# Biases of the first layer's MLP moved into the setup, and the input added by the third norm

## The chip, the cores and the metric

The kernel runs on one core of one Trainium2 chip. Time is device microseconds of one execution of the whole program; three runs of the kernel before lie between 2295.13 and 2299.04 us, the median is 2298.62. The core's engines are PE (TensorE), DVE (VectorE), ACT (ScalarE), POOL (GpSimd) and SP (SyncE, which only issues transfers). Each engine takes its instructions in order and waits on semaphores for the others.

## The reference, cut to what matters

Four layers of different kinds run one after the other over 8192 rows of 256 values (128 graphs of 64 nodes). The change is in the first:

```python
x1 = relu(_layernorm((L_norm @ x) @ Wc + bc, g1, be1)) + x
o  = attention(x1 @ Wq, x1 @ Wk, x1 @ Wv, adjacency)
x2 = _layernorm(x1 + o @ Wo + bo, g2, be2)
m  = gelu(x2 @ W1 + b1) @ W2 + b2
h  = _layernorm(x2 + m, g3, be3)
x  = _layernorm(x + h)              # of the stack, without weights
```

L_norm comes from a 64x64 matrix whose largest eigenvalue is found by 24 squarings.

## The kernel before

**Setup (lines 448 to 641).** SP loads weights and vectors. PE and DVE pass a 64x64 matrix back and forth: PE squares it (L624), DVE copies it back (L585), and after every fourth squaring, a run, PE sums a trace with a 64x128 by 64x1 product (L627) and DVE scales by its reciprocal (L581, L587). There are six runs. What DVE computes from the result (lnormT, ahatT and two rows of biases, L601 to L609) ends the setup, and a barrier of all engines follows.

**First layer (lines 644 to 947).** The rows are cut into 32 groups of 256, two 128-row tiles each. Four streams, 0 to 3, take 8 groups each, one per turn. The work on a group is a list of numbered slots:

- slot 0 and 1: product with lnormT, product with Wc (L864), add bc (L812) and statistics of the first norm (L344 bn_stats, L348 bn_aggr, two of each); POOL makes rstd (L356 and L358)
- slot 2: affine of the first norm on DVE, two L386 `(y - mean) * g` and two L391 `y * rstd + be`, one per tile, then relu and residual (L819)
- slot 3: PE transposes (L887), ACT copies the result as a rounded high part (L758), DVE makes the rest (the split, L802); POOL adds bo to x1 in a 128x512 add (L738)
- slots 4 to 10: query, key and value products in three passes (L323), scores, softmax (L823, L827 to L831 on DVE), product with the values
- slots 11 and 12: product with Wo, sum with L738's result (L836), statistics, rstd on POOL, affine of the second norm (L386 and L391 again)
- slot 13: PE transposes the second norm's result (L887), split as before; POOL adds b2 to it (L742, 128x512)
- slots 14 and 15: product with W1, gelu with b1_col as bias on ACT, product with W2, sum with L742's result (L845), statistics of the third norm
- slot 16: affine of the third norm on DVE; then POOL adds the layer's input, which SP loads again in slot 4 (L706), in a 128x512 add (L746)
- slot 17: statistics of the stack's norm on DVE, rstd and shift on POOL (L365 to L370); slot 18: ACT applies them (L376), SP stores (L709)

What runs on an engine when is set by plan0, a table that gives each slot of each engine a tick. The period is 88 ticks, the streams are shifted by lead = (0, 13, 19, 31), and weave writes the instructions of all streams out in the order of (tick - lead) modulo 88; the ticks set the order alone, not a time. PE, DVE, ACT, POOL and SP each follow their own list and meet by semaphores.

Of the kernel before, what the change touches and what calls it, by code (L numbers as in the profile page):

```python
# [122 lines left out]
def build_program(nc, ctx, t, out_rows):  # L123
# [258 lines left out]
    def ln_affine(dve, c, y, s, g, be, ready, rstd, count, ready_count=None):  # L382

        dve.wait_ge(ready, count if ready_count is None else ready_count)
        for n in range(TILES):
            c.step(dve.scalar_tensor_tensor(out=y[:, n, :], in0=y[:, n, :], scalar=ln_mv[:, s, n, 0:1], in1=g,  # L386
                                            op0=ALU.subtract, op1=ALU.mult))
        c.settle()
        dve.wait_ge(rstd, count)
        for n in range(TILES):  # L390
            ins = dve.scalar_tensor_tensor(out=y[:, n, :], in0=y[:, n, :], scalar=ln_rstd[:, s, n:n + 1], in1=be,  # L391
                                           op0=ALU.mult, op1=ALU.add)
            if n < TILES - 1:
                c.step(ins)
        return ins
# [47 lines left out]
    w0_hi = psem("w0_hi")  # L443
    pool_steps, sums_asked, spread_asked = psem("pool_steps"), psem("sums_asked"), psem("spread_asked")
# [3 lines left out]
    with nc.Block() as block:  # L448

        @block.sync  # L450
        def _(sp):
# [87 lines left out]
        def _(dve):  # L539
# [66 lines left out]
            dve.wait_ge(spread_done, 1)  # L606
            link(dve.tensor_tensor(ahatT[:], abdT, ps0(0)[:, 0:P], ALU.mult))
# [5 lines left out]
        def _(pe):  # L613
# [6 lines left out]
            with pe.Fori(0, SQUARINGS // RUN) as i:  # L620
                for r in range(RUN):
                    pe.wait_ge(p_ready, RUN * i + r + 1)
                    alone(pe, waits_passed)
                    pe.matmul(ps0(3)[0:NODES, 0:NODES], P64[0:NODES], P64[0:NODES], start=True, stop=True)\  # L624
                      .then_inc(squared, 1)
                pe.wait_ge(q_ready, i + 1)
                pe.matmul(ps0(4)[:, 0:1], ones[0:NODES, :], col[0:NODES, 12:13],  # L627
                          start=True, stop=True).then_inc(tr_ready, 1)
# [43 lines left out]
    def up_ps(s):  # L672
# [6 lines left out]
     atT_ready, up_done, gelu_ready, var2_ready, rstd2_ready, y_made, yx_ready, y_ready, y_stored) = (sems(n) for n in  # L679
# [3 lines left out]
                   "up_done", "gelu_ready", "var2_ready", "rstd2_ready", "y_made", "yx_ready", "y_ready",  # L683
# [6 lines left out]
        dve={1: 26, 2: 31, 3: 35, 6: 51, 8: 60, 11: 77, 12: 80, 13: 85, 15: 100, 16: 104, 17: 111},  # L690
        pool={1: 29, 3: 45, 11: 78, 13: 80, 15: 104, 16: 108, 17: 119},
        sp={2: 56, 4: 68, 18: 122})

    with nc.Block() as block:

        @block.sync
        def _(sp):
            ahead(sp, y_stored, by=16)

            def stage(s, slot, turn):  # L700
# [3 lines left out]
                if slot == 4:  # L704
                    sp.wait_ge(yx_ready[s], turn + 1)
# [87 lines left out]
        def _(dve):  # L793
            steps = Steps(dve, "l0_dve", {1: 1 + LN_STATS, 2: LN_AFFINE, 8: 2, 11: 1 + LN_STATS,
                                          12: LN_AFFINE - 1})
            tail = Steps(dve, "l0_dve_tail", {15: 1 + LN_STATS, 16: LN_AFFINE - 1, 17: LN_STATS})
            ahead(dve, var2_ready, by=2)

# [6 lines left out]
            def stage(s, slot, turn):  # L805
# [9 lines left out]
                if slot == 2:  # L815
                    c.step(ln_affine(dve, c, hb_t[s], s, g1, be1, var_ready[s], rstd_ready[s], 2 * turn + 1))
# [22 lines left out]
                if slot == 12:  # L839
                    ln_affine(dve, c, hb_t[s], s, g2, be2, var_ready[s], rstd_ready[s], 2 * turn + 2)\  # L840
# [1002 lines left out]
```

## Time and profile before

| what | value |
|---|---|
| median of three runs | 2298.62 us |
| span of the profiled execution, which is all of its time that the record gives | 2298.5 us |
| setup, to the first product of the layer | 0 to 43.0 us |
| first layer, to its last apply on ACT | 43.0 to 684.0 us |
| PE busy over the span | 2138.9 us (93%) |
| DVE busy | 1384.4 us (60%) |
| POOL busy | 440.6 us (19%) |

Busy is the share of the span in which an engine works on an instruction. A wait is the idle time just before an instruction, with the instruction of the other engine that released it. In the timeline "x2" stands for two instructions that follow one another, and the time is that of both. A pass is one of the matmul instructions into which PE takes a product.

### The profile page before, as it was taken

To read this page: it belongs to the slowest core of one execution; us is meant where nothing else is said; L and a number is where in the kernel's file an instruction comes from. 1 tells how busy PE (TensorE), PEld (TensorE's weight loads), DVE (VectorE), ACT (ScalarE), POOL (GpSimd) and SP (SyncE) were. 2 spreads that over 40 slices of the span, in tenths; PEclk is the share of its full clock that TensorE was granted. 3 is DMA by queue.
4 is the path that set the end of the run, shared out by engine and by line. 5 is a ranking of instruction groups with operands and counts; after the bars stand their busy time and mean duration, and the time that the engine had idled before them with its cause. 6 is when DMAs were issued, how large, how long until landed. Compare 5 with 4: busy or idle time off the path is not lost. (4 is left out here: it accounts for less than half of the span.)

```text
span 2298.5 us, 44203 instructions
## 1 busy us (share of the span) xinstructions
PE 2138.9 (93%) x17360; PEld 1878.8 (82%) x17360; DVE 1384.4 (60%) x2703; ACT 1153.9 (50%) x2183; POOL 440.6 (19%) x876
## 2 busy tenths in 40 slices
PE   4999999999969989999999999999999797979998
PEld 3888888888869978888888889988888786858886
DVE  4788788878866644443344434354443677956776
ACT  1444454355433357644444534443533565648886
POOL 3344344434430000000000000000000221014554
PEclk9999999999999999999999999999999899989999
DMA  3110111011013201000000000000000331001221
GB/s 99 34 56 19 41 50 55 9 46 55 28 40 109 63 30 37 1 19 1 1 1 19 19 1 1 1 1 1 1 1 1 114 119 60 1 28 60 79 76 51
DMA packets 76401, 81.86 MB, mean 36 GB/s; under 512 B 6544, under 2 KB 74000, under 8 KB 75408
## 3 DMA queue, kind: packets, MB, share of 16 engines
q1 hardware_dynamic: 76304, 80.51, 11.1%
q8 instruction: 67, 1.10, 0.2%
q14 instruction: 30, 0.25, 0.0%
HBM read 55.33 MB, written 25.17 MB: 35 GB/s over the span
## 5 line engine op out<-in xcount | busy, mean ns | idle before, releaser
L323 PE MATMUL ps<-R 128*128 128x256 f32 (+3 forms) x8136 | 1494.5, 344 | 38.5 <-DVE R L1545 12.9
L323 PEld LDWEIGHTS ps<-R 128*128 128x128 f32 x8136 | 1313.5, 191 | 202.1 <-DVE R L802 15.7
L1226 ACT ACTIVATE late_half<-ps,lstm_bias 128x512 f32<-128x512 f32 (+2 forms) x460 | 283.4, 669 | 382.1 <-PE ps L323 382.0
L365 POOL TENSOR_TENSOR ln_veps<-ln_mv,eps_tile 128x2 f32<-128x2 f32 x128 | 28.6, 223 | 1313.9 <-DVE ln_mv L348 1313.9
L864 PE MATMUL ps<-H 128*128 128x256 f32 x1024 | 238.3, 382 | 3.1 <-ACT H L785 1.7
L864 PEld LDWEIGHTS ps<-H 128*128 128x128 f32 x1024 | 188.9, 191 | 26.5 <-ACT H L785 1.9
L1261 DVE TENSOR_TENSOR late_half<-late_half 128x1024 f32<-128x1024 f32 (+2 forms) x32 | 37.6, 1176 | 186.4 <-ACT late_half L1226 186.4
L1223 ACT ACTIVATE late_half<-late_half 128x1024 f32<-128x1024 f32 (+2 forms) x66 | 68.1, 1032 | 124.4 <-DVE late_half L1266 78.4
L1263 DVE TENSOR_TENSOR late_half<-late_half 128x1024 f32<-128x1024 f32 (+2 forms) x32 | 37.6, 1176 | 132.6 <-ACT late_half L1226 132.6
L391 DVE SCALAR_TENSOR_TENSOR H<-H,ln_rstd 128x256 f32<-128x256 f32 x192 | 106.5, 595 | 6.8 <-POOL ln_rstd L358 3.3
L1270 DVE TENSOR_TENSOR H<-late_half 128x1024 f32<-128x1024 f32 (+2 forms) x34 | 45.9, 1349 | 89.9 <-ACT late_half L1226 89.9
L344 DVE BATCH_NORM_STATS2 ln_stats<-H 128x6 f32<-128x256 f32 x256 | 96.0, 417 | 5.3 <-POOL H L746 2.0
L1245 DVE TENSOR_TENSOR R<-H,R 128x1024 fp32r<-128x1024 f32 (+2 forms) x66 | 95.7, 1451 | 1.3 <-ACT R L1206 1.1
L1206 ACT ACTIVATE R<-H 128x1024 fp32r<-128x1024 f32 (+2 forms) x66 | 94.6, 1434 | 0.0
L368 POOL TENSOR_TENSOR ln_rstd<-ln_veps,minus_half 128x2 f32<-128x2 f32 x128 | 90.0, 703 | 10.0
L386 DVE SCALAR_TENSOR_TENSOR H<-H,ln_mv 128x256 f32<-128x256 f32 x192 | 90.6, 512 | 2.2 <-issue 1.6
L1273 DVE TENSOR_TENSOR late_half<-late_half 128x1024 f32<-128x1024 f32 (+2 forms) x32 | 37.7, 1177 | 81.2 <-ACT late_half L1226 81.2
L785 ACT ACTIVATE H<-ps,b_col 128x256 f32<-128x256 f32 x128 | 50.3, 476 | 68.4 <-PE ps L323 68.4
L348 DVE BATCH_NORM_AGGREGATE ln_mv<-ln_stats 128x2 f32<-128x6 f32 x448 | 55.7, 166 | 33.7 <-DVE ln_stats L344 19.7
L376 ACT ACTIVATE H_state<-H_state,ln_shift,ln_rstd 128x256 f32<-128x256 f32 x128 | 69.9, 602 | 11.4 <-POOL ln_shift L370 11.4
L1259 DVE TENSOR_TENSOR late_half<-late_half 128x1024 f32<-128x1024 f32 (+2 forms) x34 | 40.9, 1201 | 57.6 <-ACT late_half L1226 57.6
L356 POOL TENSOR_TENSOR ln_veps<-ln_mv,eps_tile 128x2 f32<-128x2 f32 x96 | 21.7, 226 | 269.0 <-DVE ln_mv L348 269.0
(211 smaller groups left out, 2668.7 us busy)
## 6 DMA issues: line engine op xcount, KB each, us to landing
H<-in_x SPq DMA_DIRECT2D x64, 256.0 KB, 4.1
residual<-H SPq DMA_DIRECT2D x32, 256.0 KB, 2.2
H<-residual SPq DMA_DIRECT2D x32, 256.0 KB, 4.0
arena<-residual SPq DMA_DIRECT2D x32, 256.0 KB, 2.8
residual<-arena SPq DMA_DIRECT2D x32, 256.0 KB, 2.2
H_state<-residual SPq DMA_DIRECT2D x32, 256.0 KB, 2.7
out<-H_state SPq DMA_DIRECT2D x32, 256.0 KB, 2.2
arena<-in_wih SPq DMA_DIRECT2D x4, 1024.0 KB, 4.8
```

What stands on the lines that cost most here:

```text
L323: mm = pe.matmul(out, lhsT(a), rhs(b), start=start and n == 0, stop=stop and n == len(PASSES) - 1)
L344: c.step(dve.bn_stats(ln_stats[:, s, n, :], y[:, n, :]))
L348: ins = dve.bn_aggr(ln_mv[:, s, n, :], ln_stats[:, s, n, :])
L368: c.step(pool.tensor_tensor(ln_rstd[:, s, :], ln_veps[:, s, :], minus_half[:, 0:TILES], ALU.pow))
L376: ins = act.activation(y[:, n, :], y[:, n, :], ACT.Identity, bias=ln_shift[:, s, n:n + 1], scale=ln_rstd[:, s, n:n + 1])
L386: c.step(dve.scalar_tensor_tensor(out=y[:, n, :], in0=y[:, n, :], scalar=ln_mv[:, s, n, 0:1], in1=g, op0=ALU.subtract, op1=ALU.mult))
L391: ins = dve.scalar_tensor_tensor(out=y[:, n, :], in0=y[:, n, :], scalar=ln_rstd[:, s, n:n + 1], in1=be, op0=ALU.mult, op1=ALU.add)
L864: mm = pe.matmul(out[:, n, :], src[:, k, n * P:(n + 1) * P], w[:, k, :], start=(k == 0), stop=(k == blocks - 1))
L1206: act.activation(x.as_window(xin[x.s][:, 0]), x.window(), ACT.Copy).then_inc(x_hi[x.s], 1)
L1223: act.activation(x.part(bg), x.part(cell[s]), ACT.Tanh).then_inc(tanh_ready[s], 1)
L1226: ins = act.activation(into[q][:, m, 0:x.cols], gate_ps(q, m, x.cols), ACT.Tanh if q == TANH_G else ACT.Sigmoid, bias=lstm_bias[:, x.p - 1 ...
L1245: dve.tensor_tensor(x.as_window(xin[x.s][:, 1]), x.window(), x.as_window(raw(xin[x.s][:, 0])), ALU.subtract).then_inc(x_ready[x.s], 1)
```

## The change

Three things change, all in the first layer and its setup.

1. b2 is folded. In the setup POOL adds b2 to be2, so the second norm's result already carries b2 and slot 13's add L742 is gone; L845 adds that result directly. The product with W1 sees b2 too, so PE computes W1 transposed times b2 in the setup, 8 products between the fourth and the fifth run of squarings, and DVE subtracts it from b1_col. W1 and a column form of b2 are loaded first, with a semaphore of their own.
2. The input is added by the third norm. POOL adds be3 to the reloaded input (new slot 12, 128x512), and the affine's second step takes this tile where it took be3. The add L746 is gone.
3. The statistics of the stack's norm move from slot 17 into slot 16 on DVE. In plan0 DVE's slot 17 goes, POOL's slots 13 and 16 go, its slot 12 comes at tick 86, and its slot 17 moves from tick 119 to 112.

```diff
+    b2_col = sb("b2_col", [P, KD])
...
+            for dst, name in ((W1, "W1"), (b2_col[:], "b2c")):
+                sp.dma_start(dst, t[name]).then_inc(w1_loaded, 16)
...
+            pool.tensor_tensor(be2, b2, be2, ALU.add).then_inc(row_made, 1)
...
+            dve.wait_ge(b1_made, 1)
+            link(dve.tensor_tensor(b1_col[:], b1_col[:], ps0(6)[:, 0:HID0 // P], ALU.subtract))
...
+            squarings(0, SQUARINGS // RUN - 2)
+            pe.wait_ge(w1_loaded, 2 * 16)
+            for m in range(HID0 // P):
+                for k in range(KD):
+                    mm = pe.matmul(ps0(6)[:, m:m + 1], W1[:, k, m * P:(m + 1) * P], b2_col[:, k:k + 1],
+                                   start=(k == 0), stop=(k == KD - 1))
+            mm.then_inc(b1_made, 1)
+            squarings(SQUARINGS // RUN - 2, SQUARINGS // RUN)
...
-        dve={1: 26, 2: 31, 3: 35, 6: 51, 8: 60, 11: 77, 12: 80, 13: 85, 15: 100, 16: 104, 17: 111},
-        pool={1: 29, 3: 45, 11: 78, 13: 80, 15: 104, 16: 108, 17: 119},
+        dve={1: 26, 2: 31, 3: 35, 6: 51, 8: 60, 11: 77, 12: 80, 13: 85, 15: 100, 16: 104},
+        pool={1: 29, 3: 45, 11: 78, 12: 86, 15: 104, 17: 112},
...
-                if slot == 13:
-                    pool.wait_ge(x_ready[s], 2 * turn + 2)
-                    pool.wait_ge(y_stored[s], 16 * turn + 16)
-                    pool.tensor_tensor(x2b_t[s], hb_t[s], over_tiles(b2), ALU.add).then_inc(biased_ready[s], 1)
-                if slot == 16:
-                    pool.wait_ge(y_made[s], turn + 1)
+                if slot == 12:
                     pool.wait_ge(xr0_loaded[s], 16 * turn + 16)
-                    pool.tensor_tensor(y_t[s], y_t[s], xr0_t[s], ALU.add).then_inc(yx_ready[s], 1)
+                    pool.tensor_tensor(xr0_t[s], xr0_t[s], over_tiles(be3), ALU.add).then_inc(x_be3[s], 1)
...
-                    dve.wait_ge(biased_ready[s], 2 * turn + 2)
-                    c.step(dve.tensor_tensor(y_t[s], token_major(s, 0), x2b_t[s], ALU.add))
+                    dve.wait_ge(y_stored[s], 16 * turn + 16)
+                    c.step(dve.tensor_tensor(y_t[s], token_major(s, 0), hb_t[s], ALU.add))
...
                 if slot == 16:
-                    ln_affine(dve, c, y_t[s], STREAMS + s, g3, be3, var2_ready[s], rstd2_ready[s],
+                    dve.wait_ge(x_be3[s], turn + 1)
+                    ln_affine(dve, c, y_t[s], STREAMS + s, g3, xr0_t[s], var2_ready[s], rstd2_ready[s],
                               2 * turn + 1, 2 * turn + 3).then_inc(y_made[s], 1)
-                if slot == 17:
-                    dve.wait_ge(yx_ready[s], turn + 2)
+                    c.settle()
+                    dve.wait_ge(y_made[s], turn + 2)
                     ln_statistics(dve, c, y_t[s], STREAMS + s, var2_ready[s])
```

Lines move by a few in the changed kernel: L344 and L348 become L346 and L350, L356 and L358 become L358 and L360, L386 and L391 become L388 and L393, L738 becomes L756, L802 L816, L819 L833, L845 L859; the new add is L759.

POOL's order from the second norm of stream 3 to that of stream 1, before. The digit of var_ready and x_ready is the stream:

```order
L356 TENSOR_TENSOR ln_veps<-ln_mv,eps_tile 128x2 [waits var_ready3]
L358 TENSOR_TENSOR ln_rstd<-ln_veps,minus_half 128x2 [waits l0_pool3]
L741 ISA [waits x_ready3]
L742 TENSOR_TENSOR H<-H 128x512 [waits y_stored3]
L356 TENSOR_TENSOR ln_veps<-ln_mv,eps_tile 128x2 [waits var_ready2]
L358 TENSOR_TENSOR ln_rstd<-ln_veps,minus_half 128x2 [waits l0_pool2]
L742 TENSOR_TENSOR H<-H 128x512 [waits y_stored2,x_ready2]
L356 TENSOR_TENSOR ln_veps<-ln_mv,eps_tile 128x2 [waits var_ready1]
L358 TENSOR_TENSOR ln_rstd<-ln_veps,minus_half 128x2 [waits l0_pool1]
L742 TENSOR_TENSOR H<-H 128x512 [waits y_stored1,x_ready1]
```

and now. The adds L759 wait for the input of streams 3, 2 and 1 (their semaphores took over the handles of pool_made, small_mm and small_steps from the setup):

```order
L358 TENSOR_TENSOR ln_veps<-ln_mv,eps_tile 128x2 [waits var_ready3]
L360 TENSOR_TENSOR ln_rstd<-ln_veps,minus_half 128x2 [waits l0_pool3]
L758 ISA
L759 TENSOR_TENSOR H<-H 128x512 [waits pool_made]
L358 TENSOR_TENSOR ln_veps<-ln_mv,eps_tile 128x2 [waits var_ready2]
L360 TENSOR_TENSOR ln_rstd<-ln_veps,minus_half 128x2 [waits l0_pool2]
L358 TENSOR_TENSOR ln_veps<-ln_mv,eps_tile 128x2 [waits var_ready1]
L360 TENSOR_TENSOR ln_rstd<-ln_veps,minus_half 128x2 [waits l0_pool1]
L759 TENSOR_TENSOR H<-H 128x512 [waits small_mm]
L759 TENSOR_TENSOR H<-H 128x512 [waits small_steps]
```

An add stood behind each rstd and waited for the affine of its own stream; now stream 3's add stands right behind stream 3's rstd, and those of streams 2 and 1 stand together behind stream 1's rstd, none waiting for an affine.

POOL's order a little earlier, between the first norms of stream 0 and the bo adds of streams 1 and 0, before:

```order
L356 TENSOR_TENSOR ln_veps<-ln_mv,eps_tile 128x2 [waits var_ready0]
L358 TENSOR_TENSOR ln_rstd<-ln_veps,minus_half 128x2 [waits l0_pool0]
L365 TENSOR_TENSOR ln_veps<-ln_mv,eps_tile 128x2 [waits var2_ready0]
L366 TENSOR_TENSOR ln_shift<-zeros,ln_mv 128x2
L368 TENSOR_TENSOR ln_rstd<-ln_veps,minus_half 128x2 [waits l0_pool_tail0]
L370 TENSOR_TENSOR ln_shift<-ln_shift,ln_rstd 128x2 [waits l0_pool_tail0]
L738 TENSOR_TENSOR H<-H 128x512 [waits x_ready1]
L738 TENSOR_TENSOR H<-H 128x512 [waits x_ready0]
```

and now:

```order
L367 TENSOR_TENSOR ln_veps<-ln_mv,eps_tile 128x2 [waits var2_ready0]
L368 TENSOR_TENSOR ln_shift<-zeros,ln_mv 128x2
L370 TENSOR_TENSOR ln_rstd<-ln_veps,minus_half 128x2 [waits l0_pool_tail0]
L372 TENSOR_TENSOR ln_shift<-ln_shift,ln_rstd 128x2 [waits l0_pool_tail0]
L756 TENSOR_TENSOR H<-H 128x512 [waits x_ready2]
L358 TENSOR_TENSOR ln_veps<-ln_mv,eps_tile 128x2 [waits var_ready0]
L360 TENSOR_TENSOR ln_rstd<-ln_veps,minus_half 128x2 [waits l0_pool0]
L756 TENSOR_TENSOR H<-H 128x512 [waits x_ready1]
L756 TENSOR_TENSOR H<-H 128x512 [waits x_ready0]
```

The four steps on stream 0's slot 17 (L365 to L370) stood between stream 0's rstd and stream 1's bo add; now (L367 to L372) they stand ahead of stream 2's bo add.

DVE's order at the end of a turn, from the sum that opens stream 1's third norm (L845) to stream 3's first norm of the next turn (L819), before:

```order
L845 TENSOR_TENSOR H<-ps,H 128x512
L344 BN_STATS ln_stats<-H 128x6 x2
L348 BN_AGGR ln_mv<-ln_stats 128x2 x2
L111 UNCONDITIONAL_BRANCH
L111 ISA
L386 SCALAR_TENSOR_TENSOR H<-H,ln_mv 128x256 x2
L86 ISA
L391 SCALAR_TENSOR_TENSOR H<-H,ln_rstd 128x256 x2
L86 REGISTER_ALU
L818 ISA
L819 SCALAR_TENSOR_TENSOR H<-H 128x512
```

and now, from the last statistics of stream 2, which the row ahead of these (L393) completes; L833 is the next row after:

```order
L346 BN_STATS ln_stats<-H 128x6 x2
L350 BN_AGGR ln_mv<-ln_stats 128x2 x2
L859 TENSOR_TENSOR H<-ps,H 128x512
L346 BN_STATS ln_stats<-H 128x6 x2
L350 BN_AGGR ln_mv<-ln_stats 128x2 x2
L111 UNCONDITIONAL_BRANCH
L111 ISA
L388 SCALAR_TENSOR_TENSOR H<-H,ln_mv 128x256 x2
L86 ISA
L393 SCALAR_TENSOR_TENSOR H<-H,ln_rstd 128x256 x2
L86 REGISTER_ALU
L832 ISA
```

The pair L346 and L350 of stream 2's stack norm is new ahead of stream 1's sum (L859) and so ahead of L833; before, it stood behind L819.

## Rows read from the trace of the kernel before

**Rows 1.** The page, part 1: busy us, share and instructions of each engine.

```profile
PE 2138.9 (93%) x17360; PEld 1878.8 (82%) x17360; DVE 1384.4 (60%) x2703; ACT 1153.9 (50%) x2183; POOL 440.6 (19%) x876
```

**Rows 2.** Waits of PE, 43 to 690 us: total us, times, longest us.

```profile
PE ps L323 <- DVE R L802: 12.8, 8, 1.7
PE ps L887 <- DVE H L819: 11.0, 16, 1.5
PE ps L887 <- DVE H L391: 7.3, 8, 0.9
```

**Rows 3.** Line L391 on DVE, 43 to 690 us: ns min/median/max.

```profile
L391 DVE SCALAR_TENSOR_TENSOR H<-H,ln_rstd x192: 471/484/1552, 51.6 to 678.1; 128x256 f32<-128x256 f32 x192
```

**Rows 4.** Timeline 282 to 328 us: start us, us, engine, line, [idle before].

```profile
297.34 4.60 PE L323 MATMUL ps<-R 128*128 128x256 f32 x24 [1.73 <-DVE R L802]
...
298.09 1.27 POOL L746 TENSOR_TENSOR H<-H 128x512 f32<-128x512 f32 x1
298.11 2.95 DVE L391 SCALAR_TENSOR_TENSOR H<-H,ln_rstd 128x256 f32<-128x256 f32 x2
299.32 1.45 POOL L738 TENSOR_TENSOR H<-H 128x512 f32<-128x512 f32 x1
```

**Rows 5.** Line L706, the input loads, 270 to 360 us.

```profile
L706 SPq DMA_DIRECT2D H<-in_x x4: 372/372/394, 316.4 to 319.2; - x4
...
DMA to landing us min/median/max: 3.4/4.6/4.9
```

**Rows 6.** Timeline 282 to 328 us, second affine of stream 3.

```profile
321.89 0.70 POOL L358 TENSOR_TENSOR ln_rstd<-ln_veps,minus_half 128x2 f32<-128x2 f32 x1
...
323.90 0.88 DVE L391 SCALAR_TENSOR_TENSOR H<-H,ln_rstd 128x256 f32<-128x256 f32 x2
...
324.84 0.66 PE L887 MATMUL ps<-ident,H 128*128 128x128 f32 x4 [0.92 <-DVE H L391]
```

**Rows 7.** Timeline 326 to 362 us, second affine of stream 1.

```profile
334.91 0.70 POOL L358 TENSOR_TENSOR ln_rstd<-ln_veps,minus_half 128x2 f32<-128x2 f32 x1
...
335.95 0.88 DVE L391 SCALAR_TENSOR_TENSOR H<-H,ln_rstd 128x256 f32<-128x256 f32 x2
...
337.53 0.66 PE L887 MATMUL ps<-ident,H 128*128 128x128 f32 x4
```

**Rows 8.** Timeline 326 to 362 us, the turn's boundary.

```profile
359.98 0.69 DVE L819 SCALAR_TENSOR_TENSOR H<-H 128x512 f32<-128x512 f32 x1
...
360.83 0.60 PE L887 MATMUL ps<-ident,H 128*128 128x128 f32 x4
```

**Rows 9.** Stretches: us, busy us (count) by engine, PEclk, DMA.

```profile
140.90:144.50 3.60, 3.13 (x24) 2.93 (x24) 3.56 (x4) 0.43 (x1) 3.39 (x4) 1.00 0.03 9
...
297.34:302.00 4.66, 4.66 (x25) 4.56 (x26) 4.59 (x6) 0.02 (x1) 3.35 (x4) 0.64 0.01 4
```

**Rows 10.** Timeline 130 to 150 us, first norm of stream 1.

```profile
145.42 0.66 PE L887 MATMUL ps<-ident,H 128*128 128x128 f32 x4 [1.39 <-DVE H L819]
```

**Rows 11.** Timeline 282 to 328 us, first norm of stream 0.

```profile
310.11 1.80 DVE L391 SCALAR_TENSOR_TENSOR H<-H,ln_rstd 128x256 f32<-128x256 f32 x2
...
312.68 0.66 PE L887 MATMUL ps<-ident,H 128*128 128x128 f32 x4 [0.84 <-DVE H L819]
```

**Rows 12.** Timeline 640 to 690 us, the layer's tail.

```profile
678.99 1.26 POOL L746 TENSOR_TENSOR H<-H 128x512 f32<-128x512 f32 x1
...
680.29 0.75 DVE L344 BATCH_NORM_STATS2 ln_stats<-H 128x6 f32<-128x256 f32 x2 [1.68 <-POOL H L746]
681.18 0.25 DVE L348 BATCH_NORM_AGGREGATE ln_mv<-ln_stats 128x2 f32<-128x6 f32 x2
```

**Rows 13.** Timeline 22 to 42 us, the setup.

```profile
26.08 0.58 PE L627 MATMUL ps<-arena 64*128 64x1 f32 x2
...
27.32 0.44 PE L624 MATMUL ps<-arena 64*64 64x64 f32 x2 [0.66 <-DVE arena L587]
...
37.88 0.21 DVE L595 TENSOR_TENSOR arena<-arena,ps 64x64 f32<-64x64 f32 x1 [0.87 <-PE ps L635]
```

More of the change, by code:

```diff
@@ L390, in ln_affine @@
         for n in range(TILES):
-            ins = dve.scalar_tensor_tensor(out=y[:, n, :], in0=y[:, n, :], scalar=ln_rstd[:, s, n:n + 1], in1=be,
+            ins = dve.scalar_tensor_tensor(out=y[:, n, :], in0=y[:, n, :], scalar=ln_rstd[:, s, n:n + 1], in1=be[:, n, :],
                                            op0=ALU.mult, op1=ALU.add)
@@ L619, in _, with squarings @@
               .then_inc(small_mm, 1)
[L620 to L628, printed above, removed]
+            def squarings(first, last):
+                with pe.Fori(first, last) as i:
+                    for r in range(RUN):
+                        pe.wait_ge(p_ready, RUN * i + r + 1)
+                        alone(pe, waits_passed)
+                        pe.matmul(ps0(3)[0:NODES, 0:NODES], P64[0:NODES], P64[0:NODES], start=True, stop=True)\
+                          .then_inc(squared, 1)
+                    pe.wait_ge(q_ready, i + 1)
+                    pe.matmul(ps0(4)[:, 0:1], ones[0:NODES, :], col[0:NODES, 12:13],
+                              start=True, stop=True).then_inc(tr_ready, 1)
+            squarings(0, SQUARINGS // RUN - 2)
[6 more added lines that the diff above has]
+            squarings(SQUARINGS // RUN - 2, SQUARINGS // RUN)
             pe.wait_ge(spread_asked, 1)
@@ L641, in build_program @@
     end_phase()
-    xr0, zt_words, hbuf, x1, vt, x1b, x2b = ([buf(G2) for _ in S] for _ in range(7))
+    xr0, zt_words, hbuf, x1, vt, x1b, yb = ([buf(G2) for _ in S] for _ in range(7))
     attn = [buf(HEADS * TILES, NODES) for _ in S]
     attn_pairs = [v.rearrange("p (h n) k -> p h (n k)", n=TILES) for v in attn]
-    xs_t, xr0_t, hb_t, x1_t, v_t, x1b_t, x2b_t = ([tiles_of(v) for v in b]
-                                                  for b in (xs, xr0, hbuf, x1, vt, x1b, x2b))
-    y_t = x2b_t
+    xs_t, xr0_t, hb_t, x1_t, v_t, x1b_t, y_t = ([tiles_of(v) for v in b]
+                                                  for b in (xs, xr0, hbuf, x1, vt, x1b, yb))
     zT_f = [blocks_of(v) for v in zt_words]
@@ L704, in stage @@
                 if slot == 4:
-                    sp.wait_ge(yx_ready[s], turn + 1)
+                    sp.wait_ge(y_made[s], turn + 1)
                     sp.dma_start(xr0_t[s], rows_of_group(x_rows, s, turn)).then_inc(xr0_loaded[s], 16)
@@ L795, in _ @@
                                           12: LN_AFFINE - 1})
-            tail = Steps(dve, "l0_dve_tail", {15: 1 + LN_STATS, 16: LN_AFFINE - 1, 17: LN_STATS})
+            tail = Steps(dve, "l0_dve_tail", {15: 1 + LN_STATS, 16: LN_AFFINE - 1 + LN_STATS})
             ahead(dve, var2_ready, by=2)
+            ahead(dve, y_made)
             def split_lo(s, count, half):
@@ L815, in stage @@
                 if slot == 2:
-                    c.step(ln_affine(dve, c, hb_t[s], s, g1, be1, var_ready[s], rstd_ready[s], 2 * turn + 1))
+                    c.step(ln_affine(dve, c, hb_t[s], s, g1, over_tiles(be1), var_ready[s], rstd_ready[s], 2 * turn + 1))
                     c.settle()
@@ L834, in stage @@
                     dve.wait_ge(product_done[s], 3 * turn + 2)
-                    dve.wait_ge(biased_ready[s], 2 * turn + 1)
+                    dve.wait_ge(biased_ready[s], turn + 1)
                     c.step(dve.tensor_tensor(hb_t[s], token_major(s, 0), x1b_t[s], ALU.add))
@@ L839, in stage @@
                 if slot == 12:
-                    ln_affine(dve, c, hb_t[s], s, g2, be2, var_ready[s], rstd_ready[s], 2 * turn + 2)\
+                    ln_affine(dve, c, hb_t[s], s, g2, over_tiles(be2), var_ready[s], rstd_ready[s], 2 * turn + 2)\
                         .then_inc(x_ready[s], 1)
```

14 lines of the change are left out of this document (9 added, 5 removed).

## The prediction

> **What bounds the kernel now.** I read the page's engine line first: PE is busy 93% of the span, DVE 60%, POOL 19% [rows 1]. The change touches only the setup (0 to 43 us) and the first layer (43 to 683 us), so I then asked who PE waits for there. Almost all of it is DVE: 12.8 us in 8 waits for the split L802, 11.0 us in 16 waits for the first norm's last step L819, 7.3 us in 8 waits for the second norm's affine L391 [rows 2]. A turn lasts some 78.6 us and PE is in order, with hardly a gap elsewhere, so what makes DVE later at one of these places lengthens the turn, and what makes it earlier gains at most what PE waits there. POOL matters only by what it does to DVE. I therefore looked at single instructions of one turn in the timeline. L391 takes 484 ns in the median and 1552 ns at most, 1068 ns more [rows 3]; in the timeline the long ones are those that meet a 128x512 add on POOL. At 298.09 two such adds run back to back, L746 and then L738, and a pair of L391 that normally takes 0.88 us takes 2.95, so 2.07 more; the second add started between the two halves of the pair [rows 4]. At 310.11 one L738 stretches a pair to 1.80, 0.92 more [rows 11]. So an add on POOL that asks while DVE works through an affine gets its turn between two DVE instructions and costs DVE 0.92 to 1.07 us.
>
> The Trainium skill's page SBUF — State Buffer, section SBUF: two separate sides, speaks against this change: it calls the port pair of VectorE and GpSimd an exclusive lock, held for the full instruction, and the loser fully blocks. By that the price would be the add's whole 1.28 us, 0.2 more than the rows show at each of the three collisions per turn below, some 5 us more in all. The measured 1.07 is used here.
>
> **POOL's adds: two leave, one comes.** Per stream and turn, L742 (b2) and L746 (the input) go, and an add of be3 to the loaded input comes. The adds that go cost little: L742 waits for L391 of its own norm and so starts when the affine is over. Only the L746 at 298.09 blocked an affine; that is counted below. The new add waits for no DVE result, only for the input's load. Those loads are issued at 316.4 to 319.2 and land 3.4 to 4.9 us later [rows 5], so by 321.3 for stream 3 and 324.1 at the latest for the others, but the adds stand in POOL's queue right behind the second norm's rstd.
>
> *Stream 3:* the rstd L358 ends at 322.59, the add asks for the port at once, and DVE is in L386 and L391 until 324.78 with PE's transposes L887 already waiting 0.92 us for them [rows 6]. One collision, 0.92 to 1.07: I take 1.0, in all 8 turns, **+8.0 us** (lower end 0, if the add comes late or DVE keeps the port).
>
> *Streams 2 and 1:* their two adds stand together behind stream 1's rstd, which ends at 335.61; L391 of stream 1 runs from 335.95 to 336.83, and PE takes L887 at 337.53 [rows 7]. This is the pattern of [rows 4], two adds against one affine: 2.0 us late, L391 ends at 338.83. With the 0.06 us from L391's end to L887's start that [rows 6] show, PE starts at 338.89, 1.36 late (0.70 of slack is used up). Eight turns: **+10.9 us** (ends 0 and 8 x 1.43 = 11.4). Stream 0's add falls on bn_stats and on steps that read PSUM; L746 ran beside such steps at no cost to them, so I cost it at nothing.
>
> **The statistics that move.** The outer norm's bn_stats and bn_aggr were slot 17 and now follow the third norm's affine directly. A pair costs 0.75 + 0.25 us with 0.15 between them, 1.15 [rows 12]. Number and price stay; the place moves. For stream 2 they now stand ahead of stream 1's third norm and of stream 3's first norm. L819 there ended at 360.67 and PE took L887 at 360.83 [rows 8]: a slack of 0.1, so PE starts about 1.05 later at this boundary. From there to the L819 that ends the stretch DVE has no idle time (284 to 302 in the turn before it), so I sum what changes in it. Up to the split L802 that PE waits for at 297.34: +1.15 (stream 2), -1.15 (stream 1's pair, which stood in the way before, is now done earlier), +1.15 (stream 0's pair, now ahead of the split), +0.4 (L738 of stream 3 meets L391 more squarely): the split is 1.55 late. Up to L819, which PE waits for next, -1.07 more, since the L746 at 298.09 is gone: 0.5 late. What this costs depends on the clock. After the wait of 1.73 us at 297.34 the granted clock was 0.64 (a mix of 1.2 and 2.4 GHz) and the 24 passes of L323 took 4.60 us; after the same wait at 140.90 it was 1.00 and they took 3.13 [rows 4, 9]. Seven turns have this wait, four of them the slow form. Where the clock stays up, L887 waited for L819 anyway (1.39 us, [rows 10]), and the turn loses 0.5; where it falls, PE is the later one and loses 1.55. A little further on L887 waits 0.84 us for an L819 that was blocked by L738 [rows 11]; without stream 0's slot-17 steps on POOL ahead of it, that L738 runs 1.5 us earlier, beside steps with one SBUF input, and the wait goes. The 11.0 us of [rows 2] leave some 0.5 to 0.6 for each wait that is not a 1.39; I take 0.6. Four turns x (1.55 - 0.6) + three x (0.5 - 0.6) = **+3.5 us** (ends -4 and +6.7: all turns without the boundary's delay, all turns slow).
>
> **Clock after the longer wait.** Stream 3's wait at 324.84 grows from 0.92 to 1.92 us. After 0.92 the clock never fell; 1.92 lies nearest the 1.73 us wait, after which it fell in 4 of 7. The price is 4.60 - 3.13 = 1.47. 8 x 4/7 x 1.47 = **+6.7 us** (ends 0 and 11.8).
>
> **Setup.** PE gets 8 fp32 products of 128x128 weights by one column between the fourth and fifth run of squarings, which DVE and PE pass back and forth. Nearest row: L627, 64x128 weights by one column, 0.50 us of weight loading and 0.58 in all; the next squaring starts 0.66 after PE is free [rows 13]. 8 x 0.50 - 0.66 = 3.3, and nothing covers it, since the last step of this chain ends the setup. The new subtraction on DVE is like L595, 0.21 plus a hand-over [rows 13]: 0.25. Together **+3.6** (lower end: one pass of a transpose, 0.60/4 [rows 8], 16 x 0.15 - 0.66 + 0.25 = 2.0; upper 8 x 0.58 - 0.66 + 0.25 = 4.2). POOL's add of two rows and the two column loads end long before this chain does.
>
> **Tail.** After the last product nothing covers DVE and POOL: DVE waited 1.68 us for the last L746 [rows 12]. That wait becomes a hand-over: **-1.6 us**.
>
> **Sum.** 8.0 + 10.9 + 3.5 + 6.7 + 3.6 - 1.6 = +31.1. Against the profiled span of 2298.5 us, which stands 0.1 below the median of the runs (2298.62), that gives 2329.6 us, 1.4% slower.
>
> **Rivals.** (1) *The new adds harm nothing*: a load lands late or the port goes to POOL outside the affines. Then the stream 3, stream 1 and clock terms vanish: 3.5 + 3.6 - 1.6 = +5.5, 2304. For it: stream 3's load lands as little as 1.3 us before the add. Against it: [rows 4] show who wins between two DVE instructions. (2) *DVE relieved, faster.* The place is 297 to 302: without L746 the L819 there comes 1.07 earlier; if stream 2's statistics find a gap before the boundary, the split is earlier too, the clock stays up, and a turn gains 1.07 + 0.6. With harmless adds: 7 x -1.67 + 3.6 - 1.6 = -9.7, 2288.8. The point that decides is whether the split starts before or after its old place against PE's work. For it: [rows 2, 4]; against it: DVE works without a gap from 350 to the end of the turn and on through the next boundary, so there is no idle time into which 1.15 us could go. (3) *The clock falls more often*: at all of stream 3's waits (+5.1), at the split in all turns (+3.2) and at stream 1's wait as often as at the split now (+6.7): 2345.
>
> **How the numbers follow.** My forecast has 0.62, rival 1 0.15, rival 2 0.13, rival 3 0.10. A measurement of this kernel tells about 0.2% (4.6 us) from no change. Faster by more than that is rival 2 and a sliver: 0.14. Within it lie a part of rival 1 and the forecast's lowest corner: 0.09. Slower: 0.77. The forecast alone spans 2316 to 2340: from collisions at 0.92 each with no clock term, nothing at the boundary and the lower setup, to every term at its upper end. The range of 2300 to 2347 leaves out rival 2 and thin edges.
>
> **What would show it.** Right: pairs of the second line of the affine at 1.8 us or more at stream 3 and near 2.9 at stream 1, in every turn, with a POOL add beside them; PE's wait for that line up from 7.3 us to some 26; the last statistics directly behind the last affine; a setup some 3.5 us longer. Wrong: affines of the second norm that keep 0.88, or a wait for the split that shrinks.

## The result and the profile after

| | kernel before | changed kernel |
|---|---|---|
| median (4 runs each) | 2298.66 us (2295.13 to 2299.04) | 2348.48 us (2347.32 to 2350.33) |
| ratio, 95% interval | | 1.0217, 1.0202 to 1.0232 |
| span of the profiled execution | 2298.5 us | 2345.2 us |
| setup, to the layer's first product | 43.0 us | 47.2 us |
| first layer, from there to ScalarE's first step of the second layer | 645.2 us | 673.2 us |
| recurrent stage, from ScalarE's first step in it to its first step of the next stage | 959.2 us | 972.8 us |

The change makes the kernel 2.2% slower; 1.4% was forecast, and 2348.5 lies 1.5 us above the upper end of the range. The landmarks of the timeline (the last three rows) say where: 4.2 us in the setup, 28.0 in the first layer and 13.6 in a stage that the change doesn't touch. What lies between and behind these differs by 1.3 us at most.

The page, part 1, of the changed kernel (busy us, share, instructions), to be read beside [rows 1]:

```profile
PE 2166.3 (92%) x17376; PEld 1888.5 (81%) x17376; DVE 1399.9 (60%) x2704; ACT 1152.3 (49%) x2183; POOL 401.4 (17%) x845
```

POOL has 39 us less to do, as meant. PE is 27 us *busier*, though the change gives it only 3.5 us of products. So PE's own instructions became slower somewhere.

First the part that was forecast. PE's waits in the first layer (40 to 740 us; total, times, longest), beside [rows 2]:

```profile
PE ps L902 <- DVE H L393: 24.9, 16, 1.9
PE ps L324 <- DVE R L816: 20.8, 8, 2.9
...
PE ps L902 <- DVE H L833: 6.0, 8, 1.0
```

L393, L816 and L833 are L391, L802 and L819 of the kernel before. The waits for the affine rose from 7.3 to 24.9 us, those for the split from 12.8 to 20.8; those for the first norm fell from 11.0 to 6.0. The timeline, 330 to 360 us, shows the second affines of stream 3 and of stream 1:

```profile
338.06 0.70 POOL L360 TENSOR_TENSOR ln_rstd<-ln_veps,minus_half 128x2 f32<-128x2 f32 x1
...
338.74 1.63 POOL L759 TENSOR_TENSOR H<-H 128x512 f32<-128x512 f32 x1
...
339.16 1.89 DVE L388 SCALAR_TENSOR_TENSOR H<-H,ln_mv 128x256 f32<-128x256 f32 x2
...
342.03 0.66 PE L902 MATMUL ps<-ident,H 128*128 128x128 f32 x4 [1.93 <-DVE H L393]
...
352.09 0.69 POOL L360 TENSOR_TENSOR ln_rstd<-ln_veps,minus_half 128x2 f32<-128x2 f32 x1
...
352.75 2.88 POOL L759 TENSOR_TENSOR H<-H 128x512 f32<-128x512 f32 x2
353.13 2.78 DVE L393 SCALAR_TENSOR_TENSOR H<-H,ln_rstd 128x256 f32<-128x256 f32 x2
...
355.97 0.65 PE L902 MATMUL ps<-ident,H 128*128 128x128 f32 x4 [1.18 <-DVE H L393]
```

L759 is the new add. In stream 3 it starts when the rstd L360 ends, and the pair L388 beside it takes 1.89 us where it takes 0.87 undisturbed: PE waits 1.93 us, in [rows 6] 0.92. In stream 1 two adds run back to back, and the pair L393 takes 2.78 in place of 0.88: PE waits 1.18, in [rows 7] not at all. Timeline, 300 to 320 us, the split that PE waits for longest:

```profile
312.63 0.75 DVE L346 BATCH_NORM_STATS2 ln_stats<-H 128x6 f32<-128x256 f32 x2
313.53 0.25 DVE L350 BATCH_NORM_AGGREGATE ln_mv<-ln_stats 128x2 f32<-128x6 f32 x2
313.69 0.66 DVE L816 TENSOR_TENSOR R<-ps,R 128x512 fp32r<-128x512 f32 x1
...
314.41 4.64 PE L324 MATMUL ps<-R 128*128 128x256 f32 x24 [2.88 <-DVE R L816]
```

The moved statistics (L346, L350) stand right before the split; in [rows 4] the wait there was 1.73. Three stretches behind longer waits, the first and the last of them behind stream 3's (length, busy us and count of PE, PEld, DVE, ACT and POOL, then PEclk and DMA), beside [rows 9]:

```profile
95.06:99.70 4.64, 4.64 (x45) 3.52 (x45) 2.20 (x4) 2.72 (x10) 0.00 (x0) 0.63 0.00 0
314.41:319.10 4.69, 4.69 (x26) 4.69 (x27) 4.00 (x6) 0.02 (x1) 1.99 (x3) 0.64 0.00 0
342.03:344.40 2.37, 2.37 (x16) 1.88 (x17) 1.23 (x2) 1.68 (x6) 0.00 (x0) 1.00 0.00 0
```

After 2.88 us at the split the granted clock averages 0.64, and it falls so in all seven turns that have this wait (before: four of seven). After 1.92 to 1.93 us in stream 3 it stays at 1.00 in six turns of eight; in the first (95.06) and the last (669.07) it averages 0.63. There PE needs 4.5 and 4.6 us from these transposes to the next product in three passes, where it needs 2.9 at full clock.

The setup, 22 to 48 us, beside [rows 13]:

```profile
26.82 3.57 PE L645 MATMUL ps<-b_col,H 128*128 128x1 f32 x16
...
28.84 6.01 POOL L537 TENSOR_TENSOR R<-H,R 128x512 fp32r<-128x512 f32 x4 [1.21 <-ACT R L544]
...
30.33 0.47 PE L635 MATMUL ps<-arena 64*64 64x64 f32 x2
...
32.77 2.16 DVE L585 TENSOR_TENSOR arena<-arena 64x64 f32<-64x64 f32 x1
...
47.20 1.08 PE L292 MATMUL ps<-lnormT,H 64*64 64x64 f32 x29 [4.24 <-DVEq L63]
```

In the kernel before, L585 is L577:

```profile
29.73 1.22 DVE L577 TENSOR_TENSOR arena<-arena 64x64 f32<-64x64 f32 x1
```

The 16 passes of the eight products take 3.57 us. The squaring that started at 27.32 before starts at 30.33. Counted from the trace product ahead of it (26.08 before, 26.31 now), the products delay it by 2.8 us. VectorE's L585, a step of the same chain that takes 0.22 us in the other runs of squarings, meets four subtractions on POOL (L537) in both kernels; it now takes 2.16 us, 0.94 more than before. The subtraction from b1_col brings about 0.2, and 0.2 of the 4.2 us were there before the products.

Now the part that nobody looked for. PE's products of the recurrent stage in windows of 40 us (columns: PE and PEld busy with counts, PEclk, DMA share, GB/s), first the kernel before, with 512 columns and with 462:

```profile
900.00:940.00 40.00, 40.00 (x178) 33.14 (x177) 1.00 0.00 1
1300.00:1340.00 40.00, 40.00 (x191) 35.67 (x190) 1.00 0.00 0
```

The changed kernel, the same two places:

```profile
940.00:980.00 40.00, 40.00 (x173) 32.12 (x172) 1.00 0.00 1
1350.00:1390.00 40.00, 40.00 (x196) 36.32 (x195) 1.00 0.00 1
```

PE is busy without a gap and the clock is 1.00 in both, yet 40 us hold 178 products of 512 columns before and 173 now: 225 and 231 ns each. Those of 462 columns became faster, 191 and 196.

### The profile page after: what moved, and what is told of

Its sections match the earlier page's. It is cut to its first block and busy times, and to the rows that moved or that the text cites. A ratio compares the mean times of both kernels' runs of the same rounds, so it can differ in the third digit from the quotient of the medians.

```text
span 2345.2 us, 44215 instructions
## 1 busy us (share of the span) xinstructions
PE 2166.3 (92%) x17376; PEld 1888.5 (81%) x17376; DVE 1399.9 (60%) x2704; ACT 1152.3 (49%) x2183; POOL 401.4 (17%) x845
## 3 DMA queue, kind: packets, MB, share of 16 engines
q1 hardware_dynamic: 76448, 80.51, 10.9%
## 5 line engine op out<-in xcount | busy, mean ns | idle before, releaser
L324 PE MATMUL ps<-R 128*128 128x256 f32 (+3 forms) x8136 | 1513.1, 346 | 46.3 <-DVE R L816 20.8
L367 POOL TENSOR_TENSOR ln_veps<-ln_mv,eps_tile 128x2 f32<-128x2 f32 x128 | 25.8, 201 | 1343.1 <-DVE ln_mv L350 1343.1
L879 PE MATMUL ps<-H 128*128 128x256 f32 x1024 | 243.1, 387 | 3.1 <-ACT H L798 1.7
L393 DVE SCALAR_TENSOR_TENSOR H<-H,ln_rstd 128x256 f32<-128x256 f32 x192 | 116.5, 647 | 6.6 <-POOL ln_rstd L360 3.1
L346 DVE BATCH_NORM_STATS2 ln_stats<-H 128x6 f32<-128x256 f32 x256 | 96.4, 418 | 5.8
L388 DVE SCALAR_TENSOR_TENSOR H<-H,ln_mv 128x256 f32<-128x256 f32 x192 | 94.2, 530 | 2.2 <-issue 1.6
L370 POOL TENSOR_TENSOR ln_rstd<-ln_veps,minus_half 128x2 f32<-128x2 f32 x128 | 90.8, 709 | 10.0
L358 POOL TENSOR_TENSOR ln_veps<-ln_mv,eps_tile 128x2 f32<-128x2 f32 x96 | 21.5, 224 | 403.6 <-DVE ln_mv L350 403.6
L1288 DVE TENSOR_TENSOR late_half<-late_half 128x1024 f32<-128x1024 f32 (+2 forms) x32 | 37.6, 1176 | 81.8 <-ACT late_half L1241 81.8
L350 DVE BATCH_NORM_AGGREGATE ln_mv<-ln_stats 128x2 f32<-128x6 f32 x448 | 55.6, 165 | 33.4 <-DVE ln_stats L346 16.5
```

Of the source, the lines that this page charges most:

```text
L324: mm = pe.matmul(out, lhsT(a), rhs(b), start=start and n == 0, stop=stop and n == len(PASSES) - 1)
L346: c.step(dve.bn_stats(ln_stats[:, s, n, :], y[:, n, :]))
L350: ins = dve.bn_aggr(ln_mv[:, s, n, :], ln_stats[:, s, n, :])
L370: c.step(pool.tensor_tensor(ln_rstd[:, s, :], ln_veps[:, s, :], minus_half[:, 0:TILES], ALU.pow))
L879: mm = pe.matmul(out[:, n, :], src[:, k, n * P:(n + 1) * P], w[:, k, :], start=(k == 0), stop=(k == blocks - 1))
```

## Experiments

Each kernel keeps the one that it starts from whole except for the edit shown or named. "Layer" is the first layer's length as in the table above, from each run's timeline. The kernel before had medians of 2299.7 to 2302.1 in these comparisons.

### What slowed the recurrent stage

The change allocates one more tensor, b2_col, of 8 bytes a partition, and all that is allocated behind it starts later, R2 among it, which holds the operands that the recurrent products stream. No run prints the addresses; that the shift is 32 bytes fits c1 below, whose edit shifts by 32 bytes and which gets the same product times.

```diff
     b1_col = sb("b1_col", [P, HID0 // P])
+    pad = sb("pad", [P, 2])
```

> The kernel before with one unused tensor of 8 bytes a partition where the change put its second-bias column; nothing else differs, and all tensors allocated behind it start 32 bytes later, as in the changed kernel. Theory (the recurrent stage, which the change does not touch, lost its 13.7 us to this shift of its operands): about 2312, with the 128x512 products of that stage at 173 per 40 us where the kernel before has 178, and first layer and setup as before. Rival (the stage slowed for another reason, such as where its code or transfers fall in time after a longer first layer): 2298.5, 178 per 40 us.

**2313.29 us**, ratio 1.006 (1.0043 to 1.0077): 13.6 us from a tensor that nothing uses. Products by their columns (busy us, mean ns, idle before), first the kernel before:

```profile
L323 PE MATMUL ps<-R 128*128 128x512 f32 x3312 | 755.7, 391 | 21.2 <-DVE R L1545 12.9 <-DVE R L1245 6.8 <-DVE R L1240 1.5
...
L323 PE MATMUL ps<-R 128*128 128x462 f32 x912 | 193.5, 374 | 1.1 <-DVE R L1240 1.1
L323 PE MATMUL ps<-R 128*128 128x420 f32 x456 | 88.3, 354 | 0.0
```

The kernel with the unused tensor:

```profile
L324 PE MATMUL ps<-R 128*128 128x512 f32 x3312 | 775.4, 396 | 20.9 <-DVE R L1546 12.9 <-DVE R L1246 6.8 <-DVE R L1241 1.2
...
L324 PE MATMUL ps<-R 128*128 128x462 f32 x912 | 188.9, 368 | 1.3 <-DVE R L1241 1.3
L324 PE MATMUL ps<-R 128*128 128x420 f32 x456 | 86.8, 352 | 0.0
```

+19.7 for 512 columns, -4.6 and -1.5 for the others: 13.6 us. Next, which tensor does it:

> The kernel before with the 32 bytes put in only ahead of the two tensors of the recurrent stage (R2, which its products stream, and late_half); everything that the earlier layers use stays where it was. If the place of these two sets the rate: about 2312, all of it between the start and the end of the recurrent stage. If the small tensors ahead of them do it: 2298.5.

**2315.51 us**, 1.007 (1.0043 to 1.0097), 774.4 us for 512 columns: it is R2 or late_half, not what stands ahead of them.

> The kernel before with the 32 unused bytes between R2 and late_half: the streamed operands stay, the buffers that ScalarE and VectorE work on in that stage move. Theory (the streamed operand decides): 2299.7, the 512-column products at 755 to 757 us in all. Rival (late_half decides): 2313, 775 us.

**2300.26 us**, 0.9996 (0.9981 to 1.0012), 757.1 us: moving late_half alone does nothing, so it is R2.

> The kernel before with 64 unused bytes a partition at the same place. If only a start that is a multiple of 64 matters: 2298.5, 178 products per 40 us. If any move of the tensors costs: 2312 or another value off 2298.5.

**2306.30 us**, 1.0031 (1.0018 to 1.0044), 762.4 us for 512 columns and 194.9 for 462. Neither expectation: a start at a multiple of 64 isn't enough, and the price differs from that of 32.

> The kernel before with 128 unused bytes ahead of R2 and late_half. The shift by 32 gave 775 us of 512-column products, that by 64 gave 762, none 756. If the rate goes with the start within 128 bytes: 756, 2299.7. If it goes with the start within a longer stretch: another value, 745 to 775, and the time moves with it.

**2315.11 us**, 1.0061 (1.0042 to 1.0081), 773.3 us for 512 columns, 188.9 for 462, 88.3 for 420. The rate doesn't repeat after 128 bytes either. The last of this group moves the streamed operand alone, and only in the third skip, where 462 or 420 of 512 columns are in use:

```diff
+            self.off = 8 if p == 3 else 0
...
-                                      lambda h: src[s][:, h, k, 0:x.cols], a == 0, a == len(operands) - 1)
+                                      lambda h: src[s][:, h, k, x.off:x.off + x.cols], a == 0, a == len(operands) - 1)
```

(The writers of xin and hin get the same offset.)

> The kernel before with one edit in the recurrent stage: for the third skip alone (462 and 420 columns in buffers of 512) the streamed operands xin and hin start 8 words (32 bytes) into their buffers; weights, outputs, the other tensors and the 512-column products stay where they are. Theory (the start of the operand that TensorE streams sets the rate): the 462- and 420-column products take 188.9 and 86.8 us in place of 193.5 and 88.3, as in the kernels with the 32-byte shift, so 2299.7 less 6, 2293 to 2295. Rival (another tensor that the shift moved, late_half, does it): 2299.7, 193.5 and 88.3.

**2297.11 us**, 0.9981 (0.997 to 0.9991), 4.9 us less:

```profile
L323 PE MATMUL ps<-R 128*128 128x512 f32 x3312 | 756.6, 391 | 21.2 <-DVE R L1546 12.9 <-DVE R L1246 6.9 <-DVE R L1241 1.5
...
L323 PE MATMUL ps<-R 128*128 128x462 f32 x912 | 189.0, 368 | 1.3 <-DVE R L1241 1.3
L323 PE MATMUL ps<-R 128*128 128x420 f32 x456 | 86.8, 352 | 0.0
```

The 512-column products stay, the others take the times of the 32-byte shift. So the place in SBUF of the buffers that TensorE streams sets the rate of its products: shown directly for 462 and 420 columns, and for 512 by leaving out the other tensors one after the other. Why some starts are better than others stays open. Whether it is the start by itself, or its place relative to the weights or to what ScalarE and VectorE write into the same buffers, no run separates: the writers moved along.

The change itself without that side effect, b2_col as two columns of the setup's scratch:

```diff
-    b2_col = sb("b2_col", [P, KD])
...
     col = sq(16)
+    b2_col = sq(KD)
```

> The changed kernel with the second-bias column in the setup's scratch, so that no tensor is moved; the change is otherwise whole. Theory: the 13.7 us of the recurrent stage go and the first layer keeps its loss, 2334 to 2335. Rival: 2347.

**2335.48 us**, 1.0152 (1.0123 to 1.0181), layer 672.3, 756.4 us for 512 columns. 13.0 us are back; what is left is setup and first layer. The next kernels start from this one.

### What slowed the first layer and the setup

```diff
                 if slot == 12:
+                    pool.wait_ge(x_ready[s], 2 * turn + 2)
                     pool.wait_ge(xr0_loaded[s], 16 * turn + 16)
```

> The changed kernel with the bias column in scratch (b1_after_scratch, 2335.5) and one more wait: GpSimd's new add of the input and the last bias starts only when the second norm of its stream is ready, as the removed bias add did. Theory (that add runs beside the second affine of streams 3 and 1 and stretches the affine's first instruction to 1.5 us): the waits of 1.93 us in stream 3 and of 1.18 us in stream 1 go back to 0.92 and under 0.1, some 8.0 and 9.0 us in all, so about 2318. Rival (the affine itself waits for something that the wait does not touch): 2335. A third way: the waiting add holds back GpSimd's next reciprocal, and a part of the gain is lost, 2322 to 2330.

**2313.84 us**, 1.006 (1.004 to 1.008), layer 654.0. PE's waits, 40 to 740 us:

```profile
PE ps L323 <- DVE R L817: 20.8, 8, 2.9
...
PE ps L903 <- DVE H L392: 8.7, 16, 0.9
PE ps L903 <- DVE H L834: 7.6, 9, 1.3
```

The waits for the affine fall from 24.9 to 8.7, close to the 7.3 of the kernel before; the split's stay. The layer gains 18.3 us for 16.2 us of waits, and with 0.92 us of wait the clock falls in no turn of stream 3. So the collisions made these waits, and POOL's waiting costs next to nothing: the first norm's waits grow by 0.5 us (7.1 in b1_after_scratch).

```diff
-        dve={1: 26, 2: 31, 3: 35, 6: 51, 8: 60, 11: 77, 12: 80, 13: 85, 15: 100, 16: 104},
+        dve={1: 26, 2: 31, 3: 35, 6: 51, 8: 60, 11: 77, 12: 80, 13: 85, 15: 100, 16: 104, 17: 111},
...
-                    c.settle()
+                if slot == 17:
                     dve.wait_ge(y_made[s], turn + 2)
```

> b1_after_scratch with the second statistics of the third norm put back as a step of their own on VectorE, at their old tick 111 (17). Theory (moved ahead of the next stream's split they hold it back, so that TensorE waits 2.87 us in place of 1.73 at the split and the clock falls for the 24 passes behind it in every turn, and 0.95 us at the turn's boundary): the split wait falls back toward 1.73, the boundary wait of 0.95 goes, 8 to 14 us less, 2322 to 2327. Rival (the split is late because of the collisions earlier in the turn, not because of the statistics): 2335.

**2319.50 us**, 1.0089 (1.0071 to 1.0106), layer 660.1. PE's waits, 40 to 740 us:

```profile
PE ps L902 <- DVE H L392: 24.9, 16, 1.9
...
PE ps L323 <- DVE R L816: 12.8, 8, 1.7
PE ps L902 <- DVE H L833: 10.1, 13, 1.5
```

The split's waits are those of [rows 2] again, and the 24 passes behind them are slow in two turns of seven. The first norm takes back 3 us (7.1 in b1_after_scratch). The layer gains 12.2 us: 5.0 by the sum of these waits, and the rest with the clock, since in b1_after_scratch the passes were slow in all seven turns and five times 1.5 us is 7.4.

```diff
-            squarings(0, SQUARINGS // RUN - 2)
-            pe.wait_ge(w1_loaded, 2 * 16)
-            for m in range(HID0 // P):
...
+            for i in range(SQUARINGS // RUN - 2, SQUARINGS // RUN):
+                for r in range(RUN):
...
+                    m, k = divmod(RUN * i + r - SQUARINGS + 2 * RUN, KD)
+                    mm = pe.matmul(ps0(6)[:, m:m + 1], W1[:, k, m * P:(m + 1) * P], b2_col[:, k:k + 1],
+                                   start=(k == 0), stop=(k == KD - 1))
```

> b1_after_scratch with the eight products of the setup one by one behind the last eight squarings, where TensorE waits 0.40 us for VectorE each time, in place of one row of 3.57 us between two squarings. Theory: first product of the first layer at 44.0 to 44.5 us in place of 47.2, so about 2332. Rival (the setup is later for another reason, its weight load or the subtract): 47.2 stays, 2335.

**2329.38 us**, 1.0134 (1.0114 to 1.0153). The interval meets that of b1_after_scratch, so the time alone wouldn't show it; the timeline does: the first product of the layer starts at 44.09 in place of 46.85. Some 0.7 of these 2.8 us are L585, which takes 1.33 us here and 2.02 in b1_after_scratch.

> The three edits together on b1_after_scratch: what is left of the change is the fold of the bias, the new add on GpSimd and the third norm that adds input and bias in its last step. If the losses add up: 2335.5 less 17, 10 and 3, about 2305; the removed adds of the turn's tail give 1.6 and the old wait of 0.84 in stream 0 is gone, so down to 2298 if these show. If the norm that reads the summed input costs by itself: over 2312.

**2303.06 us**, 1.0012 (1.0003 to 1.0022), layer 643.8 against 645.2 before, setup 0.8 us longer. So the three edits and the scratch column take back nearly the whole loss, and what is left of the change is worth nothing here. The single gains don't add up in the medians (21.6, 16.0 and 6.1 us against 32.4 for all); by the lengths of setup and layer they nearly do (18.3, 12.2 and 2.8 against 31.5). The four runs of b1_after_scratch spread over 7 us.

### Whether the change's own saving can be had

PE still waits 1.73 us for the split in every turn of g1_all: VectorE takes the third norm's affine of stream 0 ahead of the split of stream 2. One tick turns these two round, and moves nothing else:

```diff
-        dve={1: 26, 2: 31, 3: 35, 6: 51, 8: 60, 11: 77, 12: 80, 13: 85, 15: 100, 16: 104, 17: 111},
+        dve={1: 26, 2: 31, 3: 35, 6: 51, 8: 60, 11: 77, 12: 80, 13: 85, 15: 100, 16: 105, 17: 111},
```

> g1_all (2303.1) with the third norm's affine one tick later on VectorE (16: 104 to 105), which moves one thing in a turn: the split of stream 2 now comes ahead of the affine of stream 0's third norm in place of behind it. Theory (that affine is what the split waits for, 1.73 us in all turns, and the clock falls behind it in 4 of 7): the split wait goes to under 0.4, some of it comes back as a wait of about 1.0 for the first norm of stream 1 behind it, and the 24 passes take 3.14 us each time: 5 to 12 us less, 2291 to 2298, faster than the kernel before. Rival (VectorE is the bound there, so the 1.73 us come back whole at the next norm and the clock falls there): 2300 to 2305.

**2291.65 us**, 0.9959 (0.9947 to 0.9971), layer 630.3. Timeline, 288 to 300 us:

```profile
292.31 0.66 DVE L825 TENSOR_TENSOR R<-ps,R 128x512 fp32r<-128x512 f32 x1
...
292.88 0.87 DVE L387 SCALAR_TENSOR_TENSOR H<-H,ln_mv 128x256 f32<-128x256 f32 x2
...
293.02 3.14 PE L323 MATMUL ps<-R 128*128 128x256 f32 x24
...
293.79 0.88 DVE L392 SCALAR_TENSOR_TENSOR H<-H,ln_rstd 128x256 f32<-128x256 f32 x2
294.58 0.88 DVE L387 SCALAR_TENSOR_TENSOR H<-H,ln_mv 128x256 f32<-128x256 f32 x2
295.50 0.88 DVE L392 SCALAR_TENSOR_TENSOR H<-H,ln_rstd 128x256 f32<-128x256 f32 x2
...
296.41 0.69 DVE L842 SCALAR_TENSOR_TENSOR H<-H 128x512 f32<-128x512 f32 x1
...
297.16 0.66 PE L911 MATMUL ps<-ident,H 128*128 128x128 f32 x4 [1.00 <-DVE H L842]
```

The split (L825) ends before PE is free; of its 1.73 us, 1.00 comes back at the first norm, and the 24 passes take 3.14 us in every turn. The same tick in the kernel before:

> The kernel before with the third norm's affine one tick later on VectorE (16: 104 to 105), so that the split of stream 2 comes ahead of it, as in g2_norm_behind_split; nothing of the change is in it. If the change's arithmetic is worth nothing: 2291 to 2293, as g2. If the change gives something at the split, where GpSimd's add of the third norm's output and the input (1.80 us beside the affine) is gone: 2294 to 2300, g2 stays ahead. If the order alone gains more without the change's setup products: 2288 to 2290.

**2307.74 us**, 1.0025 (1.0013 to 1.0037), layer 650.6: slower than before, which none of the three expectations had. Timeline, 290 to 304 us:

```profile
296.61 3.14 PE L323 MATMUL ps<-R 128*128 128x256 f32 x24
...
298.67 1.52 POOL L746 TENSOR_TENSOR H<-H 128x512 f32<-128x512 f32 x1
299.09 2.79 DVE L391 SCALAR_TENSOR_TENSOR H<-H,ln_rstd 128x256 f32<-128x256 f32 x2
...
300.15 1.44 POOL L738 TENSOR_TENSOR H<-H 128x512 f32<-128x512 f32 x1
...
301.91 0.69 DVE L819 SCALAR_TENSOR_TENSOR H<-H 128x512 f32<-128x512 f32 x1
...
302.65 1.07 PE L887 MATMUL ps<-ident,H 128*128 128x128 f32 x4 [2.90 <-DVE H L819]
```

L746 is the add that the change removes. It and L738 still meet the affine L391 of the first norm, as they did before the tick (2.95 us in [rows 4]): the pair takes 2.79 us in place of 0.88. So VectorE is hardly earlier at L819, and the 1.73 us that PE no longer waits at the split come back in a wait of 2.90 us there, where g2 waits 1.00. The stretch from 302.65 on:

```profile
302.65:306.30 3.65, 3.65 (x11) 3.12 (x12) 2.15 (x6) 2.52 (x4) 0.00 (x0) 0.53 0.00 0
```

The granted clock is down to 0.53, and it falls behind this wait in all seven turns; PE's waits for split and first norm together even shrink, from 23.8 to 22.0 us. So here the reordering pays only in the kernel without POOL's last add: 16 us lie between these two kernels. That L746 causes it is read from this place, not from a kernel in which it alone differs.

> g2_norm_behind_split with the third skip's streamed operands 32 bytes into their buffers, as in c1_before_shift_p3. The two act in different stages: if they add up, 2291.7 less 5 to 6, 2285 to 2287. If the slower clock elsewhere takes it back: 2289 to 2292.

**2287.96 us**, 0.994 (0.9925 to 0.9956): the two gains add up to within their spread (3.7 us more, 5 to 6 expected). This is the fastest version, 0.6% under the kernel before.

## Why the prediction was right and wrong

- **The step that failed** is no term of the sum but its frame: "The change touches only the setup (0 to 43 us) and the first layer". With it the recurrent stage stood at nothing. The change moves what is allocated behind b2_col too, and that stage took 13.6 us more. Without that, the changed kernel takes 2335.5, 5.9 over the forecast and inside the range.
- **Stream 3, +8.0:** right. 1.93 less 0.92, eight times, is 8.1. The stretched pair was the affine's first line (L388), not its second; the pair of 1.89 against 0.87 gives 1.02. By the rule of the Trainium skill, page SBUF — State Buffer, section SBUF: two separate sides, the engine that comes second blocks until the other's instruction is over. The trace agrees: in [rows 4], at stream 1 above and in d1 the stretched pair ends 0.28 to 0.29 us after the last add ends. So the price goes with what is left of the add when VectorE asks; the prediction's reading, the whole 1.28 us each time, was too much.
- **Streams 2 and 1, +10.9:** right in kind, 9.4 measured (1.18 for 1.36), since the pair took 2.78 and not 2.95.
- **Statistics, +3.5:** too small. Over the six turns from the first of the seven long splits to the last, a turn grew from 78.3 to 81.8 us; less 1.01 and 1.18 for the collisions, 1.33 a turn stay, 9.3 in seven turns. PE waited 0.95 us at the turn's boundary (1.05 forecast) and 1.14 more at the split: from the products L864 ahead of the boundary to the passes behind the split it took 1.9 us longer (359.10 to 375.97 before, 377.52 to 396.31 now), for a split forecast 1.55 late. And the split was slow in all seven turns, where the sum had kept four; rival 3 had "at the split in all turns (+3.2)". That PE's waits for the first norm shrink behind a late split (5.0 us here) was in the forecast's working.
- **Clock behind stream 3's wait, +6.7:** too large. Taking the wait as "nearest the 1.73 us wait" gave four turns in seven, but two in eight were slow, 1.6 to 1.7 us each, 3.3 in all. That this and the statistics together come to 12.6 for 10.2 is luck: two errors of opposite sign.
- **Setup, +3.6:** 4.2 measured, and the nearness is in part luck. The products cost 2.8 for the 3.3 forecast; the stretched L585, 0.94, was not in the sum. b4 took 2.8 of the 4.2 away.
- **Tail, -1.6:** g1_all, with none of these collisions left, is 1.3 us shorter than the kernel before from the last split to ScalarE's next stage (76.2 against 77.5).
- **Rival 2, "DVE relieved, faster":** its place was right. Without L746 there is time to win at 297 to 302; g2 takes it, at 2291.7 for the 2288.8 of that rival. What kept the change from it were its own add without a wait, the moved statistics and, with these mended (g1_all, 2303.1), the third norm's affine ahead of the split. Against this rival stood that VectorE "works without a gap" from 350; it does but for 0.3 us at 358.01 and 0.15 us at a time within the statistics.

## What to carry to other kernels

Removing work from an engine paid here where its instructions sat beside the critical engine's, so place what stays: the add on GpSimd that waited for nothing started beside VectorE's next two-input step, and a wait on that step's result cost next to nothing (b2). Compare the stages that a change does *not* touch first; a few bytes of a new tensor can move an operand in SBUF, and the old kernel with the tensor alone tells at once. Where a product streams the same buffer for hundreds of microseconds, its start in SBUF is worth trying out by itself.

## What was not expected of the hardware

With PE busy without a gap and the clock at 1.00, the place of the streamed buffers changed the products' time: 512 columns took 755.7 us in all, and 775.4, 762.4 and 773.3 with R2 and other tensors 32, 64 and 128 bytes further; 462 columns 193.5, and 188.9, 194.9 and 188.9. The best place differs with the shape.

The granted clock didn't follow the length of the wait alone. After 1.92 to 1.93 us in stream 3 it stayed at 1.00 in six turns of eight and fell to 0.63 in two (the changed kernel; b1, b3 and b4 have two as well). It fell after 1.73 us at the split in four turns of seven (before, g1_all) or two of seven (b3), and after 2.87 us there in seven of seven (the changed kernel) or six of seven (b2_add_waits). What else decides stays open.
